# The end of the first graph layer with GpSimd left out: the mask and beta on VectorE, the row bias as a third product

## The reference, cut to what matters

```
msgs = where(deg > 0, agg / denom, V)          # a node without edges keeps its own value row V
out  = msgs @ Wo + bo                          # 256 x 256
r    = out + node_features                     # node_features = layernorm(x)
r    = (r - mean(r)) / sqrt(var(r) + 1e-5) * gamma + beta
x    = x + r
```

## Time and profile before

| | |
|---|---|
| median of 3 runs | 3343.25 us (3339.63 to 3352.94) |
| the profiled execution | 3334.64 us |
| its span in the trace | 3332.9 us |
| granted TensorE clock over the span, mean | 0.856 |
| `build_back` | about 1396 to 1505 us |
| what runs in it | PE 39.56, PEld 30.95, DVE 81.99, ACT 33.96, POOL 43.86 us busy of 109.00 |

### The profile page before, as it was taken

One profiled execution on the slowest core, in us unless ns is written; L12 is line 12 of the kernel. 1 busy time (PEld: TensorE's weight loads), 2 busy tenths in 40 slices (PEclk: granted clock), 3 DMA queues, 4 the chain that ended last, 5 costly groups with the idle time before them and its releaser, 6 DMA issues. The chain is left out here.

```text
span 3332.9 us, 46607 instructions
## 1 busy us (share of the span) xinstructions
PE 2510.8 (75%) x13323; PEld 1866.1 (56%) x13323; DVE 2331.0 (70%) x5608; ACT 1278.3 (38%) x4689; POOL 1484.8 (45%) x1419
## 2 busy tenths in 40 slices
PE   6666666257777777545984488888888879999997
PEld 3545555135545444233863265555555558799997
DVE  8866666279999999585872499999999962022221
ACT  1000000006666666633110266666666631233332
POOL 0677777356566566040000355545454403344442
PEclk9966666568899999777996699999999969999999
DMA  4323333767666677211000554444444461322223
GB/s 112 79 79 90 90 90 90 48 200 226 196 210 207 201 213 189 57 36 27 1 1 4 160 143 138 140 142 136 143 140 140 114 190 56 85 38 36 39 36 66
DMA packets 257606, 365.59 MB, mean 110 GB/s; under 512 B 115149, under 2 KB 170225, under 8 KB 257038
## 3 DMA queue, kind: packets, MB, share of 16 engines
q0 software_dynamic: 91456, 234.61, 26.0%
q1 hardware_dynamic: 133382, 123.25, 13.6%
q10 hardware_dynamic: 32520, 4.76, 1.4%
HBM read 331.55 MB, written 34.00 MB: 110 GB/s over the span
## 5 line engine op out<-in xcount | busy, mean ns | idle before, releaser
L1648 POOL DMA_INDIRECT g_rows<-h_d,src x416 | 401.2, 964 | 763.5 <-SPq L1595 384.2
L1312 POOL DMA_INDIRECT a_strip<-kv_d,src x416 | 404.4, 972 | 302.3 <-DVE x L1448 128.4
L326 POOL DMA_INDIRECT rec_d<-o_rec_in,o_place x392 | 403.2, 1029 | 212.0 <-issue 116.1
L1336 ACT ACTIVATE x<-a_strip,x 128x64 f32<-128x64 f32 x1664 | 408.4, 334 | 135.1 <-PE a_psv L1381 134.9
L1381 PE MATMUL a_psv<-x 128*125 128x260 f32 x832 | 285.5, 447 | 129.6 <-DVE agg L1478 119.1
L1730 PE MATMUL g_psa<-g_msg,g_hot 128*125 128x256 f32 x832 | 253.1, 430 | 119.5 <-DVE g_msg L1826 119.5
L1730 PEld LDWEIGHTS g_psa<-g_msg,g_hot 128*125 128x125 f32 x832 | 148.5, 199 | 257.7 <-DVE g_msg L1826 144.6
L1381 PEld LDWEIGHTS a_psv<-x 128*125 128x125 f32 x832 | 140.6, 201 | 209.1 <-DVE agg L1478 180.5
L410 PE MATMUL o_ps_base<-o_run,o_lo_hot_t 125*128 125x26 f32 x782 | 161.7, 358 | 118.0 <-DVE o_run L540 116.7
L1683 ACT ACTIVATE g_msg<-g_vec,g_en 128x192 f32<-128x192 f32 x416 | 155.1, 443 | 206.2 <-DVE g_vec L1812 206.2
L2599 DVE TENSOR_TENSOR e_w1s<-e_psy,e_room 128x256 f32<-128x256 f32 x56 | 23.8, 425 | 287.1 <-PE e_psy L2802 287.1
(11 more groups left out here) (436 smaller groups left out, 5423.5 us busy)
## 6 DMA issues: line engine op xcount, KB each, us to landing
a_row<-rows_d SPq DMA_DIRECT2D x104, 256.0 KB
o_row<-dst_rows_d SPq DMA_DIRECT2D x98, 256.0 KB, 4.1
o_row_lo<-lo_rows_d SPq DMA_DIRECT2D x98, 128.0 KB, 4.6
e_w<-in_L_ffn_W1p SPq DMA_DIRECT2D x8, 1024.0 KB
e_w<-in_L_ffn_W2p SPq DMA_DIRECT2D x8, 1024.0 KB
a_strip<-kv_d,src POOLq DMA_INDIRECT x416
g_rows<-h_d,src POOLq DMA_INDIRECT x416
rec_d<-o_rec_in,o_place POOLq DMA_INDIRECT x392, 2.3
```

The lines of the kernel that those rows point to most:

```text
L326: pool.indirect_dma_start(out=m.rec_d[:, :], out_offset=bass.IndirectOffsetOnAxis(ap=place[s % RP][:, u:u + 1], axis=0), in_=rec_in[:, U * ...
L1312: pool.indirect_dma_start(out=strip[:, lane.start + u, place:place + 2, :].rearrange("p a d -> p (a d)"), out_offset=None, in_=m.kv_d[:, : ...
L1336: act.activation(msg[b][:, u, h, 0:HD], strip[:, lane.start + u, place, h * HD:(h + 1) * HD], ACT.Copy, scale=w[:, k * U + u, h:h + 1])
L1648: pool.indirect_dma_start(out=rows[r][:, u, 64:576], out_offset=None, in_=m.h_d[:, :], in_offset=bass.IndirectOffsetOnAxis(ap=m.src[:, s * ...
```

## The change

What it does:

- POOL has no block in this stage any more. The mask (`v` times `dz`) becomes `masked(g)` on DVE, inside `prepare(g)`, between its product and its sum. `beta` is added to `m.x` by `shifted(g)` on DVE, right behind `spread(g)`.
- The row bias is no longer added to `nb`. `bo` is kept as one row on one partition, and each tile's two products get a third, of a row of ones (1x125) with `bo` (1x256), that accumulates into the same PSUM. `ones` is written by one memset on DVE, which PE awaits once (`s_one`). `evict` waits for `node_rows` (`s_n`) instead of `s_nb`.
- DVE awaits the parameters (`s_c`) behind `prepare(0)` and `prepare(1)` instead of ahead of them. PE's wait for them stays where it was. The load of `bo` reads 1 KB instead of 125 KB.

```diff
--- before.py
+++ after.py
@@ -709,7 +709,9 @@
             return ctx.enter_context(nc.sbuf_tensor(f"b_{name}", shape, dt))
 
         wo = sb("wo", [128, 2, D])
-        bo, gamma, beta = [sb(n, [P, D]) for n in ("bo", "gamma", "beta")]
+        gamma, beta = [sb(n, [P, D]) for n in ("gamma", "beta")]
+        bo = sb("bo", [1, D])
+        ones = sb("ones", [1, P])
         rd, dz = [sb(n, [P, NT, H]) for n in ("rd", "dz")]
         nmr0 = sb("nmr0", [P, NT])
         v, nb, y = [sb(n, [P, NT, D]) for n in ("v", "nb", "y")]
@@ -725,7 +727,7 @@
         s_div = sem("b_div")
         s_n = sem("b_n")
         s_vz = sem("b_vz")
-        s_nb = sem("b_nb")
+        s_one = sem("b_one")
         s_xb = sem("b_xb")
         s_mult = sem("b_mult")
         s_prep = sem("b_prep")
@@ -759,20 +761,6 @@
                 for p in PARTS:
                     sp.dma_start(v[p, group(g), :], v_rows[p, group(g), :]).then_inc(s_v[g], 16)
 
-        @block.gpsimd
-        def _(pool):
-            pool.wait_ge(s_c, 64)
-            pool.wait_ge(s_div, DIVIDED)
-            for g in range(NG):
-                pool.wait_ge(s_v[g], 16 * len(PARTS))
-                pool.tensor_tensor(hd(v[:, group(g), :]), hd(v[:, group(g), :]),
-                                   dz[:, group(g), :, None].to_broadcast([P, G, H, HD]), ALU.mult).then_inc(s_vz, 1)
-                pool.wait_ge(s_n, g + 1)
-                pool.tensor_tensor(nb[:, group(g), :], nb[:, group(g), :], bo[:, None, :].to_broadcast([P, G, D]), ALU.add
-                                   ).then_inc(s_nb, 1)
-                pool.tensor_tensor(m.x[:, group(g), :], m.x[:, group(g), :], beta[:, None, :].to_broadcast([P, G, D]),
-                                   ALU.add).then_inc(s_xb, 1)
-
         @block.tensor
         def _(pe):
             def turn(g, i):
@@ -793,14 +781,16 @@
                 if q >= 2:
                     pe.wait_ge(s_e, q - 1)
                 for n in range(len(tiles(g, i))):
+                    to = ps_o[q % 2][0:P, n * D:(n + 1) * D]
                     for k in range(2):
-                        last = pe.matmul(ps_o[q % 2][0:P, n * D:(n + 1) * D], rt[q % RT][:, n, k, :], wo[:, k, :],
-                                         start=k == 0, stop=k == 1)
+                        pe.matmul(to, rt[q % RT][:, n, k, :], wo[:, k, :], start=k == 0, stop=False)
+                    last = pe.matmul(to, ones[:, :], bo[:, :], start=False, stop=True)
                 last.then_inc(s_mm, 1)
 
             units = [(g, i) for g in range(NG) for i in range(UNITS)]
             turn(*units[0])
             pe.wait_ge(s_c, 64)
+            pe.wait_ge(s_one, 1)
             for q, unit in enumerate(units):
                 if q + 1 < len(units):
                     turn(*units[q + 1])
@@ -835,7 +825,7 @@
                                           scale=rs[:, j:j + 1])
                 last.then_inc(s_yn, 1)
 
-            act.dma_start(bo[:, :], vec(a["L0_gnn_bo"])).then_inc(s_c, 16)
+            act.dma_start(bo[:, :], a["L0_gnn_bo"].rearrange("(o d) -> o d", o=1)).then_inc(s_c, 16)
             act.dma_start(wo[:, :, :], half(a["L0_gnn_Wo"])).then_inc(s_c, 16)
             act.dma_start(beta[:, :], vec(a["L0_gnn_beta"])).then_inc(s_c, 16)
             act.dma_start(gamma[:, :], vec(a["L0_gnn_gamma"])).then_inc(s_c, 16)
@@ -861,18 +851,29 @@
             ch(dve.scalar_tensor_tensor(nmr0[:, :], m.mean[:, :], -1.0, m.rstd[:, :], ALU.mult, ALU.mult))
             assert ch.n == SHIFTED
 
+            def masked(g):
+                dve.wait_ge(s_v[g], 16 * len(PARTS))
+                dve.tensor_tensor(hd(v[:, group(g), :]), hd(v[:, group(g), :]),
+                                  dz[:, group(g), :, None].to_broadcast([P, G, H, HD]), ALU.mult).then_inc(s_vz, 1)
+
+            def shifted(g):
+                dve.wait_ge(s_n, g + 1)
+                dve.tensor_tensor(m.x[:, group(g), :], m.x[:, group(g), :], beta[:, None, :].to_broadcast([P, G, D]),
+                                  ALU.add).then_inc(s_xb, 1)
+
             def prepare(g):
                 if g >= 2:
                     dve.wait_ge(s_tr, UNITS * (g - 1))
                 dve.tensor_tensor(hd(slot[g % 2][:, :, :]), m.agg[:, group(g), :, 0:HD],
                                   rd[:, group(g), :, None].to_broadcast([P, G, H, HD]), ALU.mult).then_inc(s_mult, 1)
+                masked(g)
                 dve.wait_ge(s_mult, g + 1)
                 dve.wait_ge(s_vz, g + 1)
                 dve.tensor_tensor(slot[g % 2][:, :, :], slot[g % 2][:, :, :], v[:, group(g), :], ALU.add
                                   ).then_inc(s_prep, 1)
 
             def evict(g):
-                dve.wait_ge(s_nb, g + 1)
+                dve.wait_ge(s_n, g + 1)
                 for i in range(UNITS):
                     q, js = UNITS * g + i, tiles(g, i)
                     dve.wait_ge(s_mm, q + 1)
@@ -915,12 +916,14 @@
                 dve.wait_ge(s_xb, g + 1)
                 dve.tensor_tensor(m.x[:, js, :], m.x[:, js, :], y[:, js, :], ALU.add).then_inc(s_out, 1)
 
-            dve.wait_ge(s_c, 64)
+            dve.memset(ones[:, :], 1.0).then_inc(s_one, 1)
             prepare(0)
             prepare(1)
+            dve.wait_ge(s_c, 64)
             for g in range(NG):
                 evict(g)
                 spread(g)
+                shifted(g)
                 if g + 2 < NG:
                     prepare(g + 2)
                 if g == NG - 1:
```

## The result

The changed kernel takes 3354.17 us in the median of ten runs (3352.6 to 3363.09), the kernel before 3340.97 in ten (3334.44 to 3352.94). The ratio is 1.0046, with a 95% interval of 1.0032 to 1.006: some 13 to 15 us slower, where 19.5 faster was forecast. The profiled execution took 3354.57 us, with a span of 3352.8 and a mean granted clock of 0.847.

A forecast was written before the change was run, and what follows sets the result against it. DVE's chain was taken to set the end of stage `build_back`, which lies between two barriers. -25.7 - 20.9 + 12.0 + 15.1 = -19.5 us, off a median of 3343.25, gave 3324, with a range from 3320 to 3328.

The forecast's parts named there:

- POOL's departure: In stage `build_back`, five DVE instructions lose their excess time beside POOL, 25.7 us, as no POOL instruction is left.
- The start-up: At the stage's start, waits of 12.0 us replace 20.9: 8.5 and 2.0 for V rows, 1.5 in the first eviction.
- The operations added to DVE: Five masks and five beta sums on DVE, about 1.5 us each, none hidden; 15.1 us with the memset.
- The third product: On PE, two instructions a tile, 50 in all, each as long as a full product's: 0.22 or 0.44 us.
- From group 1 on it is hidden: After the first group, PE finishes products in time for DVE's evictions, which DVE reaches 6.8 us after `spread` in group 1.
- The third product is dear: Rival: on PE, switching between 128-partition and one-partition operands costs 0.4 us more a tile, 4.7 in all; 3328.5; chance 0.12.
- The clock: PE's clock rises to 2.4 GHz in group 0 and stays up over later gaps; if not, 2.8 us are lost.
- With the clock rising midway as in group 0 of before: In the first eviction, PE speeds up partway, so units 0, 1 and 2 finish at about 1417.2, 1420.1 and 1422.1.
- Slower: Rival: PE stays at 1.2 GHz and bounds the stage, 17.3 us a group from root to root; +4.8 us, 3348; chance 0.05.
- the assumption that it holds: Between groups, PE's clock stays up over a gap of about 2.5 us; if not, 2.8 us are lost.

## Why the prediction was wrong

*POOL's departure: right.* 25.7 us were to go, and every operation of DVE in the stage is at its undisturbed length in the trace after. That DVE stood for POOL before was argued from coinciding ends. It is now shown by the kernel before with the third product alone, where the operations beside POOL's instructions are long and those between them short.

*The start-up: right, mis-sized by about 1 us.* Waits for V of 9.6 us, for which I had 10.5.

*The operations added to DVE: right.* 14.9 us and a memset of 0.16, for 15.1.

*The third product: wrong, and with the clock the whole miss.* The waits for products are 35.7 us, where the sum had 1.5 in the first eviction and nothing behind it. The step is "I take what the full product takes, 0.22 or 0.44, as it has the same columns", and with it "From group 1 on it is hidden". The same columns took the same time with 65 and 128 partitions, and not with 1, 32 and 64. The one-row product costs a tile 0.42 to 0.58 us beyond that at 1.2 GHz (3.14 against 2.72 and 2.56) and 0.38 at 2.4. This is the 0.4 that the rival "The third product is dear" had, with a chance of 0.12. By the prediction's own sum it would have cost some 5 us alone.

*The clock: wrong, and by estimate the larger part.* No run has the changed kernel's work at the higher clock, so the two parts are not measured apart; the 5 us above, of 34, is what makes me call this one the larger. "With the clock rising midway as in group 0 of before" was read off a stream of full-row instructions and carried over to one broken up by others. The clock never rose while PE worked, and at 1.2 GHz a tile took 3.14 in place of some 1.7 with the passages at 2.4 (an estimate, 1.30 and 0.38). The rival "Slower" had the mechanism, PE as the bound at 1.2 GHz, with 17.3 us from root to root and +4.8 us. It lacked the passages: 17.3 and five tiles of 0.42 are 19.4, and 19.5 was measured. Five tiles in that group took 15.4 us in all, 0.43 a tile more than that rival's 2.65. I had given it 0.05, and argued against it with the clock's rise in each group before, "with less work". That was no evidence, since the added work was of another kind. What I should have weighed is that two rivals shared one cause, the operand of one partition, and add up.

With full rows the forecast's steps hold: 14.8 us of waits where I had 12.0, and a stage of 16.9 us less for 19.5. There the clock held over the first gap between groups and was down again for part of the first products in the later ones, so the assumption that it holds was half right.

The Trainium skill, TensorEngine Tiling (Array Packing), section Key Properties, says that changing the tiling mode drains TensorE. The step between 65 and 64 partitions agrees with it if operands of up to 64 partitions are placed in a smaller tile, which no trace shows. The runs give about 0.4 us as the price of going over and back, and tell only that the passage costs, not what happens in the array.

What stays open: what in the one-row products keeps the clock at 1.2 GHz. The idle weight loading between them, the rows that rest, or both would fit every kernel here. The runs show that with a third product of 1, 32 or 64 partitions the granted clock of the stage was 0.51 or 0.52, with 65 and 128 it was 0.75 and 0.77, with the one-row pairs side by side 0.60, and with doubled full-row work 0.83. They don't part these causes.

## What to carry to other kernels

A bias by a row of ones is cheap in columns and was dear here as an operand of one partition between operands of 128: give it more than 64 partitions, with zeros in the others (a stage of 91.2 us in place of 122.3), or leave it on another engine (96.9). When a change mixes operands of another height into a stream of products, don't carry over the clock of the stream before; price the stage at 1.2 GHz as well, and take rivals with a common cause as one case. And before counting a large operation on DVE at its recorded length, look whether POOL runs beside it: the smallest operations show it best (2161 ns in the mean for one that takes 165 alone).

## What the runs showed of the hardware that I had not expected

- A float32 product of 256 columns took 439 ns an instruction in the record with 65 partitions and 701 with 64, in the same place of the same kernel, and a tile with it 2.72 against 3.15 us at the same 1.2 GHz.
- More work on PE made a stage shorter: with each full product issued twice, 111.6 us in place of 122.3, at a granted clock of 0.83 in place of 0.51.
- PE's records covered 89.26 us of 122.3 at a granted clock of 0.51, and 39.56 of 108.1 before at 0.68: the larger busy share stood beside the lower clock.
- A 125x5 operation of DVE took up to 2.80 us beside POOL's operations on 125x1280, and 0.17 where POOL's stood elsewhere in time.
